# Turning the first expert's weights with SyncE's transposing DMA, and reordering around it, in a one-core decoder layer kernel

## The reference

```python
x = x + attn(layernorm(x))      # linear attention, 16 heads of 32: elu(q), elu(k), silu(v), silu(u)
                                # kv = k^T v per head; out = q kv; u * layernorm(out, g, b) @ Wo + bo
x = x + experts(layernorm(x))   # 4 experts, one per token, chosen by token id // 6250
#   the three weights of expert e are all ctx_2048[e] (512 x 512):
#   g = silu(h @ W[e].T); u = h @ W[e].T; y = (g * u) @ W[e].T
x = x + ffn(layernorm(x))       # silu(h @ q(W_up).T) * (h @ q(W_gate).T) @ q(W_down).T
#   q(w): scale = mean|w| + 1e-8; clip(round(w / scale), -1, 1) * scale     (2048 hidden)
```

## Time and profile before

| | |
|---|---|
| Time of three runs | 680.95 us median (679.29 to 681.01) |
| The profiled execution | 680.71 us; its span is 678.9 us, so 1.8 us lie around the span |
| Busy share of the span | PE 97%, DVE 74%, ACT 43%, POOL 31% |
| Mean granted TensorE clock | 0.995 of full |
| Transposing DMAs | 50, all issued by SP |

### The profile page before, as it was taken

One profiled execution on the slowest core, in us unless ns is written; L12 is line 12 of the kernel. 1 busy time (PEld: TensorE's weight loads), 2 busy tenths in 40 slices (PEclk: granted clock), 3 DMA queues, 4 the chain that ended last, 5 costly groups with the idle time before them and its releaser, 6 DMA issues.

```text
span 678.9 us, 11797 instructions
## 1 busy us (share of the span) xinstructions
PE 659.8 (97%) x4435; PEld 430.0 (63%) x4465; DVE 504.2 (74%) x818; ACT 294.8 (43%) x435; POOL 210.6 (31%) x221
## 2 busy tenths in 40 slices
PE   8989999999999979999999999999999999999996
PEld 7446546546547565555556777777777777777772
DVE  6676683773754869998986986887878886676665
ACT  4475664555545254554332533342433433332331
POOL 4032543034025300001220535326343644324222
PEclk9989999999999999999999999999999999999999
DMA  7948069059058275973320111113030211101001
GB/s 197 376 150 239 1 177 258 0 126 276 31 124 261 97 269 161 252 205 94 71 55 2 30 27 28 28 28 90 1 55 2 56 62 28 28 1 63 1 1 62
DMA packets 91444, 68.15 MB, mean 100 GB/s; under 512 B 71681, under 2 KB 71681, under 8 KB 90369
## 3 DMA queue, kind: packets, MB, share of 16 engines
q1 hardware_dynamic: 88832, 59.03, 32.4%
q0 software_dynamic: 2560, 8.42, 3.4%
HBM read 42.51 MB, written 8.41 MB: 75 GB/s over the span
## 4 chain that ended last, share of the span: by engine, by line
PE 84%; DMA 7%; SPq 3%; DVE 2%; ACT 2%; issue 1%; POOL 0%; POOLq 0%; DVEq 0%; ACTq 0%
PE bank L1350 34%; PE bank L1637 28%; PE bank L1646 15%; DMA stage<-in_L_ffn_W_up_dram 4%; PE bank L1343 3%; PE bank L1516 1%; SPq L220 1%; PE bank L1538 1%; DMA late<-n 1%; PE bank L1502 1%; ACT stage L578 1%; DMA stage<-in_L_ffn_W_gate_dram 1%; DMA stage<-in_L_ffn_W_down_dram 1%; SPq L234 0%; DMA sorted_residual<-rows,pos 0%
## 5 line engine op out<-in xcount | busy, mean ns | idle before, releaser
L1637 PE MATMUL bank<-w_att,region 128*128 128x256 f16 x1024 | 127.6, 273 | 0.0
L1646 PE MATMUL bank<-region,w_moe 128*128 128x512 bf16 x482 | 113.8, 379 | 2.3 <-DVE w_moe L1260 0.8
L1637 PEld LDWEIGHTS bank<-w_att,region 128*128 128x128 bf16 x1024 | 100.1, 98 | 18.2 <-DVE tmpA L1275 0.2
L1350 PE MATMUL bank<-late,w_att 128*128 128x512 f16 x384 | 86.2, 383 | 0.3 <-DMA late<-n 0.3
L1271 DVE TENSOR_TENSOR n<-bank,n 128x512 f32<-128x512 f32 x112 | 71.4, 685 | 18.9 <-PE bank L1637 17.1
L491 POOL TENSOR_TENSOR w_moe<-tmp,w_moe 128x512 f16<-128x512 f32 x30 | 39.2, 1307 | 139.1 <-ACT w_moe L734 139.1
L1646 PEld LDWEIGHTS bank<-region,w_moe 128*128 128x128 f16 x512 | 50.0, 98 | 48.8 <-DVE w_moe L1260 1.3
L727 ACT ACTIVATE n<-n,qs 128x512 f32<-128x512 f32 x64 | 44.5, 719 | 64.6 <-DVE n L1271 64.6
L1637 PE MATMUL bank<-w_att,late 128*128 128x256 f16 x512 | 66.4, 273 | 0.0
L1350 PEld LDWEIGHTS bank<-late,w_att 128*128 128x128 f16 x384 | 37.8, 99 | 44.3 <-issue 1.8
L1637 PEld LDWEIGHTS bank<-w_att,late 128*128 128x128 bf16 x512 | 50.0, 98 | 12.1
(11 more groups left out here) (178 smaller groups left out, 1057.5 us busy)
## 6 DMA issues: line engine op xcount, KB each, us to landing
stage<-in_L_ffn_W_up_dram SPq DMA_DIRECT2D x8, 1024.0 KB, 7.2
stage<-in_L_ffn_W_gate_dram SPq DMA_DIRECT2D x8, 1024.0 KB, 6.8
rows<-sorted_residual SPq DMA_DIRECT2D x16, 257.5 KB, 3.0
stage<-in_ctx_dram SPq DMA_DIRECT2D x4, 1024.0 KB
stage<-in_L_ffn_W_down_dram SPq DMA_DIRECT2D x4, 1024.0 KB
nrm<-in_L_ffn_W_down_dram SPq DMA_DIRECT2D x4, 1024.0 KB, 7.7
rows<-in_x_dram SPq DMA_DIRECT2D x1, 3072.0 KB, 16.2
rows<-in_x_dram SPq DMA_DIRECT2D x4, 256.0 KB, 3.5
```

What stands on the lines that cost most here:

```text
L1350: mm = pe.matmul(dst, lhs(*step), rhs(*step), start=(start and n == 0), stop=(stop and n == len(steps) - 1))
L1637: mm = pe.matmul(wk_ps[bank][:, q * H:(q + 1) * H], w[:, c + q, k * P:(k + 1) * P], x3S_part[slot][:, h, m, k], start=(h == 0 and k == 0), ...
L1646: mm = pe.matmul(ffy_ps[t][:, :], hid[:, u, h, q, (t % 2) * P:(t % 2 + 1) * P], tern[2][:, c + q], start=(begins and q == 0 and h == 0), s ...
```

## The change

Nine edits in one:

1. `ctx_part`, `ctx_hi` and `ctx_lo` are gone. Batch 0 uses `ctx_half_hi`, `ctx_half_lo` and two more transposing DMAs, like the others. The counts that the waits compare with move by one batch.
2. SP's order in batch 0 becomes that of the other batches: turn the high part, read W_gate, turn the low part, read W_down, read `ctx_2048[1]`, turn x of batch 1. Before, `ctx_2048[1]` was read after x of batch 1 had been turned.
3. In batch 0, ACT's switch to the Exp table (L636) moves ahead of the last `magnitudes`.
4. In the last batch, the four high x high matmuls of `u_part` 0 move ahead of kv; the other eight stay.
5. `two_signs(0, True)` on DVE moves ahead of `last_sum(3)`.
6. The dummy matmuls around the first `unit_transposes` become 14 and 66, from 52 and 16.
7. In step 0 of the experts, `negative(0)` moves from ahead of the step to behind `xs_lo(1)`, and the low part of the hidden tile goes ahead of `xs_lo(2)`.
8. Tiles 14 and 15 are turned by SP, not PE: `tile_turned` runs to 15.
9. With that, `xs_hi`, `xs_lo` and `xs_norm` of tiles 14 and 15 come in the regular steps (12, 13; norm 11, 12).

```diff
         def weights(b):
-            if b > 0:
-                weights_turned(b, 0)
+            weights_turned(b, 0)
             sp.wait_ge(s["abs_done"], 3 * b + 1)
             summed_unit(b, 1)
-            if b > 0:
-                weights_turned(b, 1)
+            weights_turned(b, 1)
             sp.wait_ge(s["abs_done"], 3 * b + 2)
             summed_unit(b, 2)
-            if b > 0 and b + 1 < B:
+            if b + 1 < B:
                 expert_weights(b + 1)
-            if b + 1 < B:
                 batch_turned(b + 1)
-            if b == 0:
-                sp.wait_ge(s["ctx_mm"], 4)
-                expert_weights(1)
-            if b + 1 < B:
                 sp.wait_ge(s["abs_done"], 3 * b + 3)
                 summed_unit(b + 1, 0)
...
-        for i in range(3, NT - 2):
+        for i in range(3, NT):
             tile_turned(i)
...
             if first:
-                ctx_hi(b, 0)
+                ctx_half_hi(b, last)
             if last:
                 return
             magnitudes(b, 0 if first else 1)
             act.wait_ge(s["a_mul"], K * b)
             for m in range(K):
                 u_act(b, m)
-                if first and m < 3:
-                    ctx_hi(b, m + 1)
...
+            act.wait_ge(s["exp_loaded"], b)
+            act.activation(spare[:, :], cols[:, 0, 0:1], ACT.Exp).then_inc(s["exp_loaded"], 1)
             if first:
                 magnitudes(b, 2)
-            act.wait_ge(s["exp_loaded"], b)
-            act.activation(spare[:, :], cols[:, 0, 0:1], ACT.Exp).then_inc(s["exp_loaded"], 1)
             o_copies(b)
...
                 routing_starts()
-                ctx_lo(b, 0)
                 routing_bases()
+                ctx_half_lo(b, last)
                 dve.wait_ge(s["x_rest"], 16)
...
         last_sum(2)
+        two_signs(0, True)
         last_sum(3)
-        two_signs(0, True)
...
-            if i == 0 or i + 1 in (NT - 2, NT - 1):
-                xs_lo(i + 1)
-            if i + 2 < NT - 2:
+            if i == 0:
+                xs_lo(1)
+                negative(0)
+                hidden_lo(0)
+            if i + 2 < NT:
                 xs_lo(i + 2)
-            if i + 2 in (NT - 2, NT - 1):
-                xs_norm(i + 2)
-            elif i + 3 < NT - 2:
+            if i + 3 < NT:
                 xs_norm(i + 3)
...
         xs_norm(2)
-        negative(0)
         for i in range(STEPS):
             expert_step(i)
...
-            if not last:
+            if last:
+                u_part(b, 0, first, [(0, 0)])
+            else:
                 for m in range(K):
                     u_part(b, m, first)
-                    if first and m < 3:
-                        ctx_part(b, m + 1)
...
-        u_part(B - 1, 0, False)
+        u_part(B - 1, 0, False, REST)
...
-        keep_busy(ps[0], 52)
+        keep_busy(ps[0], 14)
         unit_transposes(0, 0)
-        keep_busy(ps[0], 16)
+        keep_busy(ps[0], 66)
         unit_transposes(0, 1)
...
-            if i == 0 or i + 1 in (NT - 2, NT - 1):
-                xs_transpose(i + 1)
             if i == 0:
+                xs_transpose(1)
                 xs_transpose(2)
```

## The result

The changed kernel takes 684.43 us (median of six runs, 684.10 to 688.05); the kernel before, run beside it on the same chip, 680.63 us. The ratio is 1.0071, with a 95% interval of 1.0054 to 1.0087: slower by 4.8 us, where I had forecast 2.7 us less.

The account below looks back on a forecast made before the run. PE, busy 97%, bounds the kernel, except batch 0's chain of reads until 58.34. Terms 0.0 - 1.0 - 1.0 - 0.9 = -2.9, with 0.2 given back, make -2.7: 678.0, as median 678.2 us; range 676.6 to 680.8.

Parts of the forecast that it names:

- Steps 12 to 14, "-0.9": Expert steps 12 to 14: without PE's extra transposes each takes 5.62 us, a gain of 0.9 us.
- DVE's step 12 now has work for 5.7 us, but its hidden low part is done 0.3 us ahead of PE: Expert step 12: DVE, though fuller, would still deliver the hidden low part 0.3 us before PE needs it.
- Filling DVE and SP costs nothing: Batch 0: added DVE and SP work delays nothing; kv mask held to about 54.0, o due on ACT at 56.3.
- win nothing: Batch 0: PE's freed 1.6 + 1.4 us bring no gain by themselves, since PE is not on the chain.
- the half-clock rival: Batch 0: PE stands 2.7 us, then runs at half clock, costing 0.5 to 1.4 us more; 679.2, chance 0.16.
- Edit 3, "-1.5": Batch 0: table switch fits before W_down lands, so o's third group starts at 56.9, not 58.34: 1.5 us gained.
- high half 58.9, low half 61.7 plus the notice: Batch 0: landing times of batch 1's x behind the `ctx_2048[1]` read, eating the 1.5 us; sum 0.0.
- The queue "in order": Batch 0: DMA transfers go one after the other, so the chain of reads keeps its times; last Abs ends 56.3.
- the mark of the shared queue: Batch 0: W_gate landing later than 47.1 would show DMA engines sharing themselves out; chance of that rival 0.09.
- The rival's 681.9: Batch 0: DMA engines share out, not in order, costing 4.0 us net on the chain of reads; chance 0.09.
- The passage, "-1.0": Passage to stage 2: with signs moved ahead, POOL's last root takes 0.55 us, not 1.53; last scatter 1.0 us earlier.
- Step 0, "-1.0": Expert step 0: hidden tile's product runs before `negative(0)`, so `first(1)` starts 1.0 us earlier; bounds -0.5 and -1.1.

Follow-up runs that it names:

- mid: Kernel before plus four u matmuls ahead of kv, signs ahead of the last residual, 14 and 66 dummies, step 0 reordered: 679.72 us, ratio 0.9984.
- turn_only: `late_pe_order` with ACT's switch to Exp back behind the last Abs: 681.32 us, ratio 1.0013.
- late_pe_order: Changed kernel with tiles 14 and 15 turned by PE again and batch 0's `ctx_2048[1]` read behind x's turns: 680.78 us, ratio 1.0001.
- late_pe: Changed kernel with tiles 14 and 15 turned by PE again and their ACT and DVE work back in place: 682.95 us, ratio 1.0035.
- last2: Kernel before with only tiles 14 and 15 turned by SP, their work in the regular steps: 683.29 us, ratio 1.0043.
- wsum: Changed kernel with DVE's weight sum of step 12 moved behind the product of step 13: 682.65 us, ratio 1.0033.
- busy: `late_pe_order` with 60 dummy matmuls on PE ahead of o in batch 0: 679.04 us, ratio 0.9969.
- mid_exp: `mid` with ACT's switch to Exp moved ahead of the last Abs in batch 0: 677.64 us, ratio 0.9955.
- mid_exp_b: `mid_exp` timed once more, as partner on the same chip for the third group: 677.86 us, ratio 0.9964.
- read_first: `mid_exp` with `ctx_2048[1]` read ahead of x's turns, PE still turning the first weights: 681.65 us, ratio 1.0026.
- order: Changed kernel with `ctx_2048[1]` read behind x's turns in batch 0, as before: 683.30 us, ratio 1.0040.
- best2: `mid_exp` plus tiles 14 and 15 turned by SP and step 12's weight sum moved to the end of step 13: 679.27 us, ratio 0.9982.

## Why the prediction was wrong, point by point

The kernels form one path from the kernel before to the changed one, an edit or group at a time. A difference of two ratios times 680.6 us is the step's size; with the intervals above, each is good to about 1 us. Of the 7.5 us between the forecast (-2.7) and the measurement (+4.8), batch 0 makes 3.5 and steps 12 to 14 make 3.3.

| step | from, to | ratio to before | measured, us | predicted, us |
|---|---|---|---|---|
| edits 4 to 7 | before, `mid` | 1.0000, 0.9984 | -1.1 | -2.0 |
| edit 1 | `mid`, `turn_only` | 0.9984, 1.0013 | +2.0 | 0 |
| edit 3 | `turn_only`, `late_pe_order` | 1.0013, 1.0001 | -0.8 | -1.5 |
| edit 2 | `late_pe_order`, `late_pe` | 1.0001, 1.0035 | +2.3 | +1.5 |
| edits 8, 9 | `late_pe`, after | 1.0035, 1.0071 | +2.4 | -0.9 |

- **Steps 12 to 14, "-0.9" (wrong sign, +2.4).** The step that failed is "DVE's step 12 now has work for 5.7 us, but its hidden low part is done 0.3 us ahead of PE". I added DVE's durations as they stood and did not ask what POOL does meanwhile. The lock that I used for the roots in the passage stood unused for the sum of signs, 0.4 us away from POOL's long instruction in the kernel before. `last2` shows the collision alone, `wsum` takes it out of the product's way and with it the loss. Even the 0.3 us were not there: PE waited 0.42 for the hidden low part.
- **Batch 0, "Filling DVE and SP costs nothing", and PE's freed time, to "win nothing" (wrong, +2.0).** The freed time was no gain, as argued, but a price: PE stood 4.33 us, not the 2.7 of the half-clock rival, and o ran at 1.2 GHz. That rival had 16 in 100 and came true, with 1.6 us for its 0.5 to 1.4 (o's end in `late_pe_order` against `late_pe`; q's start in `turn_only` against `mid`). In the changed kernel's own profile the late x hides it: PE waited for the low half until 64.64 anyway. I had set a wait of 1.22 us after which PE kept its pace against it, when the stand to come was over twice as long by my own sum. The Trainium skill's rule, named in the prediction, was right here (page "TensorE: Matmul & The Clock Gate", section "Part 1: The HAM clock gate"): the granted clock was 0.50 after the stand of 4.33 us, and with the dummies of `busy` it stayed at 1.00. And filling DVE did cost: by the late statistics and POOL's step of 2.12 us, the kv mask came 0.74 us late, which lengthened the stand.
- **Edit 3, "-1.5" (right mechanism, hidden by edit 1).** Alone it gives 2.0 (`mid` to `mid_exp`, and 1.4 by the ratio of `mid_exp_b`). On top of edit 1 it gives 0.8 at most, within what the runs can tell from nothing: PE's o starts at 55.46 with and without it, held by the kv mask and then by the clock, no longer by ACT. That it is hidden is read from these times; no run has edits 1 and 3 with the clock kept and the reads on time.
- **Edit 2, "high half 58.9, low half 61.7 plus the notice" (right mechanism, mis-sized).** I saw that the read would eat the gain, but priced it by the turns' bytes, one behind the other at 2.85 us. What the runs showed is SP held 5.0 to 5.7 us in the first turn's issue whenever the read of `ctx_2048[1]` lay in front (the changed kernel, `late_pe`, `wsum`, `read_first`), against 1.3 to 2.7 with W_down's alone, so the second could not be issued until 58.5; it landed at 64.64. The high half itself landed 7.0 to 9.1 us after its issue in these four, against 4.3 to 4.5 in the kernel before, `mid` and `turn_only`; in `late_pe` and `read_first` it was the one that q waited for. The price is 2.3 us behind edit 1 and 3.8 us in `read_first`, where nothing else hides it.
- **The queue "in order" (half right).** In the changed kernel's profile W_gate landed 6.6 us after its issue, not 5.24, later than the 47.1 that I had named as the mark of the shared queue. But the low half's turn cost it 1.3 us and not 2.85, W_down's read took 4.9 with `ctx_2048[1]` behind it, and the last Abs began 0.8 us late, not 4. In `turn_only` W_gate took 5.6 us and the last Abs was not late at all, so the shared queue is not what edit 1 costs. The rival's 681.9 was the nearest forecast to the time, by another mechanism. (Its own terms, 678.2 and 4.0, add up to 682.2.)
- **The passage, "-1.0" (cause right, gain not there in `mid`).** The long root was the collision with the signs: it moved with them. The scatter behind it then took 1.67 us longer to land in `mid`, with the instruction packet in its way. In the changed kernel, which came to the passage 3.8 us late, the passage and step 0 together were 1.5 us shorter, from the first root (229.72 and 233.51) to `first(1)`.
- **Step 0, "-1.0" (right).** 1.1, from `first(0)` to `first(1)`, in `mid` and in the changed kernel.
- **Batch 1, not in the prediction (+1.9 in the one profile).** SP's second turn of x of batch 2 took 6.4, 6.3 and 6.0 us in the changed kernel, `turn_only` and `late_pe`, which turn the first weights by SP, and 4.2 and 4.0 in the kernel before and `mid_exp_b`. The instructions around it are the same, four scatters of POOL among them. `busy`, which has edit 1 too, took 4.7, so it is not the turning of the weights as such. What differs is when the instruction packet comes, as the last section shows. What it costs in the medians is inside edit 1's +2.0. In the profiles of `mid` and `turn_only` batch 0 loses 1.6 us and batch 1 another 1.0, but 1.0 comes back by `first(1)`, where the packet no longer holds the last scatter; stage 3 starts 1.7 later. That the packet is the cause is argued from its times, since no run moved it alone.

## What to carry to other kernels

An instruction that moves by half a microsecond changes which engine comes first to a shared resource: before moving one on DVE, list what POOL runs within a few microseconds of each of its neighbours, and see who would wait. Taking work from an engine that already waits is not free, since the longer stand can cost it its clock; fill the gap or leave the work there. A transposing DMA belongs ahead of the large reads in its queue, and the queue engine's own instruction time is a term of the sum. And when the same instructions take a different time in two kernels, look at the instruction queue in the list of DMA queues too: an edit also moves the moments of its packets, which by their name are the program's own text.

## What the hardware showed that I had not expected

- SP's transposing instruction is not a mere issue: with a read in flight ahead of it, it lasted about until that read had landed. It ended at 58.44 with `ctx_2048[1]` landing at 58.5 (changed kernel), at 57.85 with 57.9 (`read_first`), at 47.83 with W_gate at 48.10 (changed kernel), and at 54.77 with W_down at 54.49 (`mid_exp_b`). Its length there, 1.3 to 5.7 us for the same 512 KB, follows from when it is issued, and all that SP has behind it waits along. A read ahead is not the only thing that holds it: the two of batch 1 took 3.4 and 4.2 us in the kernel before, where the last read had landed before they were issued.
- DVE and POOL exclude one another for whole instructions in cases far from alike: a bf16 sum of 128 x 2048 (4.46 for 1.22 us), a float32 subtraction of 128 x 512 (2.93 for 0.68), and, the other way, a small one of POOL's: its 128 x 4 step of the variance at 45.53 took 2.12 us beside DVE's 2.26 us split of a weight at 45.29, where it takes 0.25 alone, and stood on the chain of batch 0.
- In `wsum` as in the changed kernel, DVE's product with one operand in PSUM (`tmpA<-bank,tmpA`, 0.68 us at 333.75 in the latter) ran across POOL's start at its usual length.
- While PE waited for x of batch 2 in the changed kernel, the DMA engines moved 12 GB/s in 117 to 118 us: the end of that wait was not bytes of its own transfer. The 16 KB instruction packet of 115.3 is the likely cause. In the six kernels where it began in 113.4 to 115.3, inside SP's second turn of batch 1 (the changed kernel, `late_pe`, `order`, `late_pe_order`, `turn_only`, `wsum`), that turn took 5.6 to 6.5 us. In the other eight it began in 98.2 to 106.5, before the turn, which took 3.8 to 4.7. In the same way the last scatter of the passage landed 4.3 to 5.2 us after its issue in the five kernels where the packet fell on it (`mid`, `mid_exp`, `mid_exp_b`, `read_first`, `best2`): in each, 3 to 5 of its 80 packets began only as the instruction packet ended. In the kernel before and `last2` it took 3.1 and 3.4.
